# ScalarE copies the queries out of PSUM, and a tile's last rows go in one copy of 2048 columns

## What is computed

```python
p_w = jnp.exp(log_p + log_tw)
phi = k_val[..., None] * theta
re_k = jnp.cos(phi)
im_k = jnp.sin(phi)
den = jnp.cumsum(p_w[..., 0], axis=1)
num_re = jnp.cumsum(pwb * re_k, axis=1)
num_im = jnp.cumsum(pwb * im_k, axis=1)
...
out_re = jnp.sum(s_re * qr + s_im * qi, axis=-1)
out_im = jnp.sum(s_im * qr - s_re * qi, axis=-1)
...
x = _layernorm(x + y @ W_out)
x = _layernorm(x + ffn(x))        # top 2 of 8 experts, and one shared expert
```

## Time and profile before

| | |
|---|---|
| Median of 3 runs | 497.6 us (496.3 to 498.78) |
| Span of the profiled execution | 519.4 us |
| Busy: PE, DVE, ACT, POOL | 89%, 70%, 68%, 56% of the span |
| Memory loop, tiles 4 to 28 | 60.7 to 211.0 us from the start |
| VectorE and ScalarE busy from 140 to 160 us | 19.90 and 19.32 us of 20 |

### The profile page before, as it was taken

The page is one execution under the profiler, slowest core; times in us unless marked ns, Lnnn a source line. Parts: engine busy times, 40 slices in busy tenths (PEclk is TensorE's granted clock), DMA queues, the critical chain, the costliest instruction groups (busy, mean ns, idle before and its releaser), DMA issues.

```text
span 519.4 us, 7568 instructions
## 1 busy us (share of the span) xinstructions
PE 462.2 (89%) x2192; PEld 299.7 (58%) x2192; DVE 362.2 (70%) x843; ACT 354.0 (68%) x551; POOL 292.5 (56%) x248
## 2 busy tenths in 40 slices
PE   8897999999999988878597877869999999999984
PEld 4333344443333333446375655658999999899732
DVE  7887999999999999997667715354343334465246
ACT  3889799999999999816244625516767666566507
POOL 3473667877787778827565563521545455655400
PEclk9997999999999999999698987989999999999998
DMA  7031226664343433001111010121222221222095
GB/s 261 3 108 55 82 76 208 221 237 146 124 147 124 147 125 145 3 1 44 41 42 42 32 51 17 42 77 42 69 77 78 67 67 57 59 62 60 16 319 166
DMA packets 41192, 48.55 MB, mean 93 GB/s; under 512 B 5616, under 2 KB 25266, under 8 KB 41152
## 3 DMA queue, kind: packets, MB, share of 16 engines
q1 hardware_dynamic: 35792, 39.07, 23.0%
q0 software_dynamic: 5216, 8.70, 5.3%
q10 hardware_dynamic: 144, 0.31, 0.2%
HBM read 19.17 MB, written 29.11 MB: 93 GB/s over the span
## 4 chain that ended last, share of the span: by engine, by line
PE 36%; DVE 36%; issue 9%; ACT 8%; another core or an unknown queue 5%; POOL 3%; DMA 2%; DVEq 0%; SPq 0%; POOLq 0%; ACTq 0%
PE routed_ph L1438 13%; PE routed_po L1451 12%; DVE memory_y_raw L753 9%; DVE memory_prod L744 9%; DVE memory_feat L729 4%; PE memory_nsum L596 3%; POOL table_scratch L1129 2%; PE routed_px L1426 2%; ACT finish_xo L1645 2%; PE dispatch_spo L960 1%; ACT memory_feat L376 1%; PE dispatch_sph L950 1%; DVE dispatch_xrow L1197 1%; DMA finish_pick<-pick_scratch 1%
## 5 line engine op out<-in xcount | busy, mean ns | idle before, releaser
L479 POOL TENSOR_TENSOR memory_feat<-memory_feat,memory_p_tok 128x1024 f32<-128x1024 f32 x64 | 121.8, 1934 | 46.2 <-ACT memory_feat L387 45.2
L596 PE MATMUL memory_nsum<-memory_feat,tri 128*128 128x512 f32 x256 | 116.9, 599 | 6.6 <-ACT memory_last_rows L396 3.6
L1414 POOL DMA_INDIRECT pick_scratch<-routed_ob,routed_xg x71 | 71.3, 1005 | 78.0 <-DVE routed_ob L1535 57.7
L1129 POOL DMA_INDIRECT table_scratch<-dispatch_xrow,dispatch_slot x64 | 61.8, 966 | 47.9 <-DVE dispatch_slot L1232 25.8
L596 PEld LDWEIGHTS memory_nsum<-memory_feat,tri 128*128 128x128 f32 x256 | 47.5, 191 | 65.3 <-issue 54.5
L1484 ACT ACTIVATE routed_rel<-routed_ph 128x512 f32<-128x512 f32 x71 | 42.3, 597 | 47.5 <-PE routed_ph L1438 46.3
L1438 PE MATMUL routed_ph<-routed_xs,routed_w1c 128*128 128x256 f32 (+1 forms) x368 | 71.2, 337 | 2.1 <-ACT routed_xs L1475 1.3
L1451 PE MATMUL routed_po<-routed_w2c,routed_hid 128*128 128x128 f32 x568 | 71.2, 275 | 0.5 <-ACT routed_hid L1493 0.5
L1535 DVE TENSOR_SCALAR routed_ob<-routed_po,routed_xg 128x128 f32<-128x128 f32 x71 | 22.6, 348 | 68.9 <-issue 47.4
L744 DVE TENSOR_TENSOR memory_prod<-memory_nsum,memory_query 128x1024 f32<-128x1024 f32 x58 | 68.3, 1215 | 1.0 <-PE memory_nsum L596 1.0
L1451 PEld LDWEIGHTS routed_po<-routed_w2c,routed_hid 128*128 128x128 f32 x568 | 67.0, 192 | 0.9 <-ACT routed_hid L1493 0.7
(11 more groups left out here) (188 smaller groups left out, 652.8 us busy)
## 6 DMA issues: line engine op xcount, KB each, us to landing
table_scratch<-memory_blank SPq DMA_DIRECT2D x68, 260.0 KB, 2.6
finish_pick<-pick_scratch SPq DMA_DIRECT2D x16, 256.0 KB, 5.8
routed_xg<-table_scratch SPq DMA_DIRECT2D x25, 130.0 KB
w<-w_up SPq DMA_DIRECT2D x9, 256.0 KB, 2.7
w<-w_down SPq DMA_DIRECT2D x9, 256.0 KB, 3.2
x_tok<-x SPq DMA_DIRECT2D x4, 512.0 KB, 3.7
out<-finish_xo SPq DMA_DIRECT2D x7, 256.0 KB, 2.3
routed_xg<-table_scratch SPq DMA_DIRECT2D x21, 65.0 KB
```

The costliest lines, as they stand in the source:

```text
L479: nc.gpsimd.tensor_tensor(v, v, pv, ALU.mult).then_inc(wfeat_done, 1)
L596: last = nc.tensor.matmul(nsum[:, o:o + 512], tri[:], feat[:, i % U, h, q * 512:(q + 1) * 512], start=True, stop=True)
L1129: nc.gpsimd.indirect_dma_start(out=table, in_=xrow[:, r, n, :], in_offset=None, out_offset=bass.IndirectOffsetOnAxis(ap=slot[:, r, n:n + 1 ...
L1414: nc.gpsimd.indirect_dma_start(out=pick_dram, in_=ob[:, u, h, :], in_offset=None, out_offset=bass.IndirectOffsetOnAxis(ap=xg[:, t % XU, h, ...
```

## The change

VectorE's `q_part` goes from the loop (the first, ahead of the loop, and the last, at tile 28, stay). ScalarE gets `keep_q(n)`, the same copy of 128 x 512, in odd tiles i = 2n - 1 between the cosine of i+2 and the last rows of i. It waits until the queries are in `pq`, and until the products of the tiles that used the query buffer before are done. `last_row(i)` is now one copy of 32 x 2048; it waits for both products. `rows_kept` counts once per tile, and both halves of the next tile's sums wait for it.

```diff
@@ -387,14 +387,19 @@
                 nc.scalar.activation(feat[:, i % U, 1], feat[:, i % U, 1], ACT.Sin, scale=-TURN, bias=half_pi[:]
                                      ).then_inc(feat_done, 1)
 
-            def last_row(i, h):
+            def last_row(i):
 
                 b = i % B
-                act.wait_ge(prod_done, 2 * i + 1 + h)
+                act.wait_ge(prod_done, 2 * i + 2)
                 if i >= B:
                     act.wait_ge(carried[b], 16 * (i // B))
-                nc.scalar.copy(last_rows[32 * b:32 * b + 32, h * NF:(h + 1) * NF], nsum[96:P, h * NF:(h + 1) * NF]
-                               ).then_inc(rows_kept, 1)
+                nc.scalar.copy(last_rows[32 * b:32 * b + 32, :], nsum[96:P, :]).then_inc(rows_kept, 1)
+
+            def keep_q(n):
+                act.wait_ge(q_done, n + 1)
+                if n >= 2:
+                    act.wait_ge(prod_done, 4 * n - 4)
+                nc.scalar.copy(query[:, n % 2].rearrange("p u c -> p (u c)"), pq_v).then_inc(q_kept, 1)
 
             act.wait_ge(soft_in, 1)
             nc.scalar.activation(sp[:, 1:2], sp[:, 0:1], ACT.Exp).then_inc(soft_exp, 1)
@@ -431,9 +436,10 @@
                 if i in (6, 8):
                     keep_p(i // 2 - 2)
                 tail(i)
+                if i % 2 == 1 and i + 3 < NT:
+                    keep_q((i + 1) // 2)
                 if i < NT - B:
-                    last_row(i, 0)
-                    last_row(i, 1)
+                    last_row(i)
                 if i == 1:
                     exp_p(1)
                     exp_p(2)
@@ -482,7 +488,7 @@
 
                 b = i % B
                 pool.wait_ge(wfeat_done, 2 * i + 2)
-                pool.wait_ge(rows_kept, 2 * (i - B) + 2)
+                pool.wait_ge(rows_kept, i - B + 1)
                 nc.gpsimd.sem_inc(carry_due, 1)
                 pool.dma_start(feat[0:1, i % U].rearrange("p h c -> p (h c)"), last_rows[32 * b + 31:32 * b + 32, :],
                                accum_op=ALU.add).then_inc(carried[b], 16)
@@ -590,7 +596,7 @@
                     if i:
                         pe.wait_ge(prod_done, 2 * i - 1 + h)
                         if i <= NT - B:
-                            pe.wait_ge(rows_kept, 2 * i - 1 + h)
+                            pe.wait_ge(rows_kept, i)
                     for q in range(2):
                         o = h * NF + q * 512
                         last = nc.tensor.matmul(nsum[:, o:o + 512], tri[:], feat[:, i % U, h, q * 512:(q + 1) * 512],
@@ -773,8 +779,6 @@
             q_part(0)
             for i in range(NT):
                 j, b = i // B, i % B
-                if b % 2 == 0 and 0 < i < NT - 2:
-                    q_part(i // 2)
                 if i == 0:
                     read_out(0, (0,))
                 if i + 3 < NT:
```

## The result

| | before | after |
|---|---|---|
| Median of the runs | 497.62 us (496.3 to 498.78) | 514.66 us (513.63 to 515.85) |
| Ratio, 95% interval | | 1.0338 [1.0313, 1.0363] |
| Products of tile 4 to products of tile 28 | 60.67 to 211.03: 150.36 us | 60.14 to 226.96: 166.82 us |
| From the products of tile 31 (230.00, 246.49) to the end | 289.4 us | 265.7 us |

The execution of the kernel before that was profiled was slow behind the memory loop (289.4 us there; the second run of the kernel that only moves the query copies, with the same code in that stage, takes 265.8), which is why its span is above that of the slower kernel. Inside the loop the same turn of four tiles comes back at 24.85 to 24.86 us, so the two kernels are compared there.

The account below looks back on a forecast made before the run. The prediction took three full engines, paced by VectorE's queue at 6.265 us per tile, as the loop's bound before; afterwards a serial 6.88 us turn through nsum. 14.8 + 0.5 + 0.25 + 0.9 = 16.4 us gave 514 us, range 509 to 519.

Parts of the forecast that it names:

- a ring through the one `nsum` buffer: In the memory loop, sums, second product, whole last-row copy and next sums follow in series: 6.265 to 6.88 us per tile.
- The turn, 6.88 us: From one tile's sums to the next: 3.63 to second product, 1.25 to copy, 1.86 copy, 0.14 to sums.
- The copy of 2048 columns, 1.86 us: ScalarE's single last-row copy, estimated from the 1024-column copy's 1.005 us plus 0.85 us for 1024 more columns.
- The tiles with a turning, 0.5 us: Four tiles where TensorE also turns denominators or weights: it comes last by 0.05 to 0.55 us, 0.5 in all.
- The edges, +0.25 and +0.9 us: Lateness of the first tiles before tile 4, 0.25 us, and of tile 29's products after tile 28, 0.9 us.
- ScalarE's floor: Rival: ScalarE's queue sets the loop's pace, 24.81 us per four tiles against 24.85; no change, 497.6 us; chance 0.04.
- The query copy behind nobody: Sign on ScalarE in the loop: the moved query copies take 0.58 us each and nobody waits for them.
- Gain: Rival: VectorE's queue alone paces the loop, -7.2 us, 490.4; needs a last-row copy under 0.89 us; chance 0.03.
- no change: Rival: ScalarE's queue paces the loop, 497.6 us; needs 6.2 us from sums to sums, copy 1.2; chance 0.04.
- the second condition: For an unchanged time, the loop would need 6.2 us from sums to sums and a last-row copy of 1.2 us.
- the second ring: Rival: copy, rounding, fraction and products through ScalarE and VectorE pace the loop, 6.45 us per tile, 503 us; chance 0.05.
- The clock did fall: Rival: TensorE, idling more in the loop, drops to its lower clock, about 9 us more, 523 us; chance 0.04.

Follow-up runs that it names:

- the form with two copies: Against the kernel before, only the query copies moved to ScalarE, last rows still in two copies of 1024 columns: loop 152.12 us, ratios 1.0055 and 1.005.
- With 1024 columns: Against the changed kernel, only the first 1024 of the 2048 last-row columns copied and carried: loop 153.45 us, ratio 1.0022 to the kernel before.

## Why the prediction was right

The forecast was 514.0 us for 514.66, and the loop stands as it said: a ring through the one `nsum` buffer. Point by point:

- *The turn, 6.88 us.* Measured 6.97. The term that was mis-sized is the first one, 3.63 us from the sums to the second product; it is 3.71, since the sums of the changed loop take 3.67 us and not 3.60. Both lengths stood in the rows (behind a wait, against the earlier trace rows), and the shorter was taken. Over 24 tiles that is some 2 us too little: the loop grew by 16.5 where 14.8 was put.
- *The copy of 2048 columns, 1.86 us*, between ends of 1.71 and 2.01: measured 1.858. The height of the output (32 partitions or 128) has no part in it: at 32 partitions 1024, 1536 and 2048 columns took 1.006, 1.432 and 1.859 us, one line of 0.83 ns a column, and this line gives 0.58 us for 512 columns, as the copies at 128 partitions took. The estimate from the Trainium skill's price (ScalarE: Activation LUTs, "What ACT_TABLE_LOAD costs"), 1.89 us, is 0.03 us above the measurement.
- *The tiles with a turning, 0.5 us.* Measured nothing. In tile 9 TensorE does the turning, phases, keys and queries from 88.96 to 92.43, 3.47 us, and is on time to a hundredth. The 3.38 us without the turning contained a gap ahead of the queries (the idle 0.26 us at 101.86) that tile 11 of the kernel before happened to have the earlier trace rows; here the same work takes 2.94 (89.49 to 92.43). This term was put from a row that was not typical.
- *The edges, +0.25 and +0.9 us.* In the profiled pair the changed kernel is 0.53 us ahead at the products of tile 4, but this pair doesn't measure the change there. In the execution before, TensorE was at its lower clock from 45 to 50 us:

```profile
45.00:50.00 5.00, 5.00 (x10) 2.19 (x9) 4.97 (x4) 4.95 (x7) 3.65 (x2) 0.50 0.32 105
```

VectorE then waited 0.75 us for the sums of tile 3, which took 4.03 us. The kernel whose sums wait for both copies has the VectorE queue of the kernel before and no such wait, and starts tile 4 at 59.81 us; against that the changed kernel is 0.33 us behind, near the 0.25. Behind tile 28 the next products come 6.94 us later instead of 5.55, 1.4 more. The "3.2 us" that the forecast started from is in no row: it was 5.55. TensorE's 6.64 us from sums to sums stayed (224.87 to 231.51), and what changed is that VectorE, no longer late, has the products of tile 28 2.09 us behind their sums instead of 3.49. Then 0.8 is given back before tile 31. Together this is 0.0 by the profiled pair and 0.9 by the cleaner one, where 1.15 was put.
- *ScalarE's floor.* 24.81 us per four tiles with the whole change could not be seen behind the ring, but the form with two copies was: 25.09 for 25.05.
- *The query copy behind nobody.* Right: 14 copies of 0.57 to 0.59 us, no one waited for them, and ScalarE still idled 0.18 us (before 139.22) even in the tile that also has a keys' copy.
- *VectorE.* Forecast: 0.7 us idle before the fraction and 0.3 before the second product; measured 0.65 and 0.39.
- *The rivals.* Gain and no change would have needed a copy under 0.89 or 1.2 us. With 1024 columns (1.00 us) the ratio is 1.0022 [0.9997, 1.0048], no change, as the second condition says; four undisturbed tiles take 25.17 us (139.96 to 165.13) against 24.85. TensorE comes next there: between the ring and VectorE's 5.91 there stood a third bound at 6.4 to 6.5 in every second tile, which the condition for the gain left out. A loop paced by the second ring, 6.45 us a tile, did not come, as the second product did wait for the sums (0.39 us before 75.23). The clock did fall, in one of the two profiled executions of the changed kernel, but at 1 us in the loop and not 9. The rule to spread the emptying of PSUM over both engines (the Trainium skill, TensorEngine Tiling (Array Packing), "PSUM Bottleneck") gave no gain here: both engines already did it, and both were full.

So the mechanism was right, and the hit to 0.7 us is partly luck: by the profiled pair the turn was 1.7 us too small, and the turning and the edges 1.65 us too large.

## What to carry over

Where several engines share one buffer, follow one tile through it and add up only what must come one after the other; that sum, and not the load of the fullest engine, is the pace as soon as it is the longer one. Two short copies, each released by its own half, were worth more here than one cheaper long copy, because the first half's buffer is free one product and one copy earlier. Before taking work off a full engine, work out how full the next two are: here the 1.2 us less on VectorE per four tiles could by the queues have given 0.04 us of them (24.81 against 24.85), and with two copies on ScalarE not even that (25.05).

## What was not expected of the hardware

TensorE's granted clock can fall from its upper level (1.00, 2.4 GHz) towards its lower one (0.50, 1.2 GHz) for one tile inside a loop that otherwise has 1.00, at a place that differs from execution to execution. In the changed kernel run again it is the first sums shown here, after an idle 1.94 us, and the stretch around it has a mean clock of 0.83:

```profile
57.56 5.37 PE L602 MATMUL memory_nsum<-memory_feat,tri 128*128 128x512 f32 x8 [1.94 <-ACT memory_last_rows L396]
...
66.23 3.67 PE L602 MATMUL memory_nsum<-memory_feat,tri 128*128 128x512 f32 x8
```

```profile
55.00:65.00 10.00, 8.06 (x20) 3.21 (x19) 8.44 (x8) 6.58 (x6) 7.35 (x5) 0.83 0.19 53
```

These sums take 5.37 us instead of 3.67, and the ring passes all of it on: 8.67 us to the next ones. In the first execution the same sums, idle for 1.72 us before, kept the upper level. With one copy alone it happened once near 200 us (clock 0.83 from 195 to 205); with both copies waited for, it was 0.90 and 0.92 from 190 to 210. The first row below is the one copy alone, the second the changed kernel in its first execution:

```profile
197.53 5.37 PE L600 MATMUL memory_nsum<-memory_feat,tri 128*128 128x512 f32 x8 [2.24 <-ACT memory_last_rows L396]
```

```profile
196.99 3.67 PE L602 MATMUL memory_nsum<-memory_feat,tri 128*128 128x512 f32 x8 [2.24 <-ACT memory_last_rows L396]
```

From 55 us on it shows in seven of the eight traces in which the sums wait for a copy in turn after turn, and in none of the four with a full loop (the kernel before, the queries alone twice, every second query copy), whose clock is 1.00 from 60 to 215 us. Each time it is one group of sums of 5.37 us behind an idle 1.79 to 2.30 us. Such an idle time is not enough by itself: behind the same 2.24 us the first execution of the changed kernel kept the upper level three times. The forecast had given the fall 0.04 and a price of 9 us; it came in most of these kernels, at 1 to 2 us each. What else must come together is left open.
